# A second layer fed in groups of 1, 1, 2, 2 and 2 row tiles, with all engines' orders rewritten there

## The reference

```python
def _L1_ffn_ref(x, w_gate, w_up, w_down, up_reorder_index, down_reorder_index):
    xf = x.reshape(B * S, H)                                       # 1024 rows of 256
    qx, sx, sc = _reorder_quantize_x(xf, up_reorder_index)         # row scale, e4m3 rounding
    g = _qlinear(qx, sx, sc, w_gate, up_reorder_index, out_idx=down_reorder_index)
    u = _qlinear(qx, sx, sc, w_up, up_reorder_index, out_idx=down_reorder_index)
    t = jax.nn.silu(g) * u                                         # 1024 rows of 704
    qt, st, sct = _reorder_quantize_x(t, down_reorder_index)
    return _qlinear(qt, st, sct, w_down, down_reorder_index).reshape(B, S, H)
x = x + _L1_ffn_ref(_L1_cond_ref(x, ...), ...)                     # cond: sigmoid(x) * ratio
```

## Time and profile before

| | |
|---|---|
| runs | 673.81 us median of 3 (673.74 to 676.32) |
| profiled execution | 671.21 us, of which its span is 669.3 us |
| granted TensorE clock, mean | 0.93 |
| busy in the span | PE 508.7, DVE 511.1, ACT 356.4, POOL 262.0 us |

### The profile page before, as it was taken

How to read it: one execution, slowest core, us unless ns; L and a number is a source line. 1 busy time by engine, 2 the same in 40 slices (tenths; PEclk the granted TensorE clock), 3 DMA queues, 4 the chain that set the end, 5 groups by cost and what they waited for, 6 DMA issues and landing times.

```text
span 669.3 us, 9350 instructions
## 1 busy us (share of the span) xinstructions
PE 508.7 (76%) x3050; PEld 347.1 (52%) x3050; DVE 511.1 (76%) x964; ACT 356.4 (53%) x758; POOL 262.0 (39%) x212
## 2 busy tenths in 40 slices
PE   2011298799999999997489989899999998046663
PEld 1000133478888888876146646566656665024432
DVE  4999867788888888874459769869798787379772
ACT  3226235777777778763054545644734564256542
POOL 4465014744444445415460872633350600630001
PEclk9999999899999999997599979999999999577785
DMA  8200003030000000004903831441453100210000
GB/s 278 96 0 0 0 1 125 27 140 1 1 1 1 1 1 25 9 1 144 292 25 107 269 58 36 163 101 43 164 147 116 25 24 16 82 53 8 17 17 24
DMA packets 28363, 44.24 MB, mean 66 GB/s; under 512 B 4795, under 2 KB 21435, under 8 KB 28059
## 3 DMA queue, kind: packets, MB, share of 16 engines
q1 hardware_dynamic: 20843, 31.43, 14.2%
q0 software_dynamic: 3072, 8.14, 5.3%
q10 hardware_dynamic: 4400, 4.06, 1.8%
HBM read 38.51 MB, written 5.12 MB: 65 GB/s over the span
## 4 chain that ended last, share of the span: by engine, by line
PE 50%; DVE 26%; ACT 8%; issue 8%; POOL 5%; DMA 1%; SPq 0%; DVEq 0%; ACTq 0%; POOLq 0%; PEldq 0%
PE pw L419 9%; PE pb L419 8%; PE pb L607 7%; PE sc L460 5%; PE sc L607 5%; PE po L419 4%; PE pt L471 3%; DVE areg L1104 2%; PE sc L683 2%; PE pb L683 2%; DVE areg L1090 2%; DVE areg L1088 2%; PE pt L616 1%; POOL breg L1668 1%; DVE areg L1451 1%
## 5 line engine op out<-in xcount | busy, mean ns | idle before, releaser
L607 PE MATMUL pb<-wreg,areg 128*128 x184 | 83.7, 598 | 0.9 <-ACT areg L925 0.8
L1640 POOL TENSOR_TENSOR breg<-breg,con 128x512 f32<-128x512 f32 x32 | 40.7, 1271 | 80.3 <-ACT breg L824 80.3
L419 PE MATMUL pw<-areg 128*128 128x256 f16 x406 | 58.8, 280 | 7.7 <-DVE areg L1459 7.7
L607 PE MATMUL sc<-wreg,areg 128*128 x184 | 63.2, 486 | 0.0
L419 PE MATMUL pb<-areg,wreg 128*128 128x512 f16 x240 | 58.9, 382 | 2.0 <-ACT breg L824 1.9
L832 ACT ACTIVATE breg<-breg,mx 128x128 f32<-128x128 f32 (+1 forms) x128 | 56.6, 446 | 1.6 <-DVE mx L1212 1.6
L460 PE MATMUL sc<-areg,breg 128*128 128x128 f32 (+1 forms) x256 | 48.8, 335 | 5.6 <-DVE mx L1212 4.3
L607 PEld LDWEIGHTS pb<-wreg,areg 128*128 128x128 f32 x184 | 33.6, 193 | 35.4 <-issue 35.1
L419 PEld LDWEIGHTS pw<-areg 128*128 128x128 f16 x406 | 40.3, 100 | 17.9 <-DVE areg L1459 11.2
L1635 POOL TENSOR_TENSOR breg<-breg 128x512 f32<-128x512 f32 x32 | 44.4, 1388 | 4.5
L460 PEld LDWEIGHTS sc<-areg,breg 128*128 128x128 f32 x256 | 38.9, 195 | 13.2 <-POOL breg L1635 4.2
(11 more groups left out here) (247 smaller groups left out, 1293.8 us busy)
## 6 DMA issues: line engine op xcount, KB each, us to landing
wreg<-in_L_ffn_w SPq DMA_DIRECT2D x24, 896.0 KB, 8.5
ys_dram<-areg ACTq DMA_DIRECT2D x23, 128.0 KB, 1.7
wreg<-in_L_ffn_wq SPq DMA_DIRECT2D x1, 2048.0 KB, 8.6
wreg<-in_L_ffn_wo SPq DMA_DIRECT2D x1, 2048.0 KB, 8.3
areg<-in_fside_BxSxS ACTq DMA_DIRECT2D x4, 256.0 KB, 5.4
x_in<-in_x SPq DMA_DIRECT2D x4, 256.0 KB, 3.9
h_dram<-areg SPq DMA_DIRECT2D x8, 128.0 KB, 1.7
out_dram<-areg SPq DMA_DIRECT2D x8, 128.0 KB, 1.7
```

The source lines that it names most:

```text
L419: last = nc.tensor.matmul(bank, w(a), m(b), start=first and k == 0, stop=final and k == 2)
L607: last = nc.tensor.matmul(bank, xsT[:, parity, c * P:(c + 1) * P], wreg[:, bass.ds(base + (m * C + c) * FF + lo, w)], start=c == 0, stop=c ...
L1640: G.tensor_tensor(t2[:, parity, :].rearrange("p (b n) -> p b n", b=2), t2[:, parity, :].rearrange("p (b n) -> p b n", b=2), rope_sin.rearr ...
```

## The change

The rows of the second layer come in five groups, of 1, 1, 2, 2 and 2 row tiles, in place of four pairs. Each group has its own semaphore for its gathers, and GpSimd issues all gathers without a wait between them. The sigmoid and the mixed input get buffers for all eight tiles; qxT, qtT, tscaled and traised are doubled. TensorE no longer follows one loop: gate and up products are two functions, the first three tiles have an order of their own, and from tile 3 on a pass holds the products of tile i, the inner transposes of tile i - 2 and the down products of tile i - 3. Products of zeros stand in six places of TensorE's order. ScalarE's and VectorE's orders are written out anew, and ScalarE takes one silu of a single column ahead of tile 2. In the first layer, one half of the last ratio piece moves: TensorE makes it in the last expert tile's pass, in the bank po, where no next tile's transposes stand.

```diff
+GROUPS = ((0, 1), (1, 1), (2, 2), (4, 2), (6, 2))
-        qxT = cut(areg, 4736, D // 2, F16).rearrange("p (c n) -> p c n", c=C)
+        qxT = cut(areg, 8576, D, F16).rearrange("p (k c n) -> p k c n", k=2, c=C)
...
-                      19: piece(down, 1, 0), 22: piece(ratio, 3, 0), 23: piece(ratio, 3, 1)}
+                      19: piece(down, 1, 0), 22: piece(ratio, 3, 1)}
...
                 if n + 1 < MT:
                     x_transposes(n + 1, (n + 1) % 4, x_slot.get(n))
+                elif n < MT:
+                    pe.wait_ge(s["xT_copied"], MT)
+                    ratio_piece(B - 1, 0, po).then_inc(s["xT_done"], 1)
...
+            pe.wait_ge(s["hTlo_done"], MT)
+            pe.wait_ge(s["x1_ready"], 1)
+            keep_clock(pt2[:, 1, :], 10)
+            quantised_transposes(0)
+            gate_products(0)
+            quantised_transposes(1)
+            up_products(0)
+            gate_products(1)
+            up_products(1)
+            keep_clock(pt2[:, 1, :], 10)
+            inner_transposes(0)
+            keep_clock(pt2[:, 1, :], 16)
+            quantised_transposes(2)
+            gate_products(2)
+            up_products(2)
+            quantised_transposes(3)
+            for i in range(3, NT):
+                gate_products(i)
+                up_products(i)
+                if i + 1 < NT:
+                    quantised_transposes(i + 1)
+                inner_transposes(i - 2)
+                down_quantised(i - 3)
+                keep_clock(pt2[:, 1, :], 2)
+            inner_transposes(NT - 2)
+            down_quantised(NT - 3)
+            keep_clock(pt2[:, 1, :], 3)
+            down_quantised(NT - 2)
+            inner_transposes(NT - 1)
+            keep_clock(pt2[:, 1, :], 4)
+            down_quantised(NT - 1)
...
             def copy_qxT(i):
                 act.wait_ge(s["qxT_done"], i + 1)
-                if i >= 1:
-                    act.wait_ge(s["upp_done"], i)
+                if i >= 2:
+                    act.wait_ge(s["upp_done"], i - 1)
...
             input_gate(0)
             scaled_input(0)
             input_gate(1)
+            copy_qxT(0)
             scaled_input(1)
-            input_gate(2)
-            copy_qxT(0)
             gate_of_tile(0)
             copy_qxT(1)
             gate_of_tile(1)
...
+            scaled_inner(0)
+            input_gate(2)
+            scaled_inner(1)
+            copy_qtT(0)
+            scaled_input(2)
+            input_gate(3)
+            input_gate(4)
+            nc.scalar.activation(tf[:, 1, 0:1], ident[:, 0:1], ACT.Silu)
+            copy_qxT(2)
+            gate_of_tile(2)
+            copy_qxT(3)
+            scaled_input(3)
+            gate_of_tile(3)
+            scaled_inner(2)
+            copy_qxT(4)
+            copy_qtT(1)
+            scaled_input(4)
+            for j in range(2, NT):
+                if j + 1 < NT:
+                    scaled_inner(j + 1)
+                if j + 2 < NT:
+                    gate_of_tile(j + 2)
+                if j + 3 < NT:
+                    copy_qxT(j + 3)
+                copy_qtT(j)
...
             mix_input(1)
+            round_input(1)
             combine(2)
-            round_input(1)
             inner_rows(0)
...
+            inner_rows(1)
+            round_inner(0)
+            mix_input(2)
+            combine(3)
+            combine(4)
+            round_input(2)
+            round_inner(1)
+            mix_input(3)
+            inner_rows(2)
+            mix_input(4)
+            round_input(3)
+            inner_rows(3)
+            round_inner(2)
+            output_rows(0)
+            round_input(4)
+            for i in range(4, NT):
+                inner_rows(i)
+                round_inner(i - 1)
+                output_rows(i - 3)
+            round_inner(NT - 1)
+            for i in range(NT - 3, NT):
+                output_rows(i)
...
-            gather_pair(0)
-            gather_pair(1)
-            for p in range(2):
-                pool.wait_ge(s_g[p], 64)
-                gather_pair(p + 2)
+            for g in range(len(GROUPS)):
+                gather_group(g)
```

More of the change, by code:

```diff
@@ L660, in quantised_transposes @@
             def quantised_transposes(i):
-                pe.wait_ge(s["qx_ready"], i // 2 + 1)
+                group = [g for g, (first, count) in enumerate(GROUPS) if first <= i < first + count][0]
+                pe.wait_ge(s["qx_ready"], group + 1)
                 if i >= 1:
@@ L668, in quantised_transposes, with first_products, gate_products @@
                 last.then_inc(s["qxT_done"], 1)
-            def gate_up(i):
+            def first_products(i, m):
+                for k in range(2):
+                    bank = (sc2[:, k] if m == 0 else pb[k])[:, 0:IH]
+                    for c in range(C):
+                        for a in range(2):
+                            last = nc.tensor.matmul(bank, qxT[:, i % 2, c, :], w_fold[m][:, a, c, k * IH:(k + 1) * IH],
+                                                    start=c == 0 and a == 0, stop=c == C - 1 and a == 1)
+                last.then_inc(s["gatep_done" if m == 0 else "upp_done"], 1)
+            def gate_products(i):
                 pe.wait_ge(s["qxT_copied"], i + 1)
@@ L675, in gate_up, with up_products @@
                     pe.wait_ge(s["inner_b_done"], MT)
[L676 to L685, removed]
+                first_products(i, 0)
+            def up_products(i):
+                if i >= 1:
+                    pe.wait_ge(s["inner_ready"], i)
+                first_products(i, 1)
             def inner_transposes(i):
@@ L1011, in gate_of_tile @@
                 act.wait_ge(s["gatep_done"], i + 1)
+                group = [g for g, (first, count) in enumerate(GROUPS) if first <= i < first + count][0]
+                act.wait_ge(s["xout_ready"], group + 1)
                 if i >= 2:
@@ L1018, in scaled_inner, with copy_qtT @@
                 act.wait_ge(s["inv_ready"], i + 1)
[L1019 to L1022, removed]
+                if i >= 2:
+                    act.wait_ge(s["qt_ready"], i - 1)
+                nc.scalar.activation(tscaled[i % 2], tvals[i % 2], ACT.Copy, scale=rs[:, 8, i:i + 1])
+                nc.scalar.activation(traised[i % 2], tvals[i % 2], ACT.Copy, scale=rs[:, 9, i:i + 1]).then_inc(s["scaled_ready"], 1)
+            def copy_qtT(i):
+                act.wait_ge(s["qtT_done"], i + 1)
+                if i >= 2:
+                    act.wait_ge(s["dn_done"], i - 1)
+                nc.scalar.copy(qtT[i % 2][0:IQ, :, :], pt2[0:IQ, 0, :].bitcast(F16).rearrange("p (c n) -> p c n", c=NI)).then_inc(s["qtT_copied"], 1)
             input_gate(0)
@@ L1548, in round_inner @@
                     dve.wait_ge(s["qtT_done"], i)
-                nearest_e4m3(qt[:, :], tscaled, traised, tgrid).then_inc(s["qt_ready"], 1)
+                nearest_e4m3(qt[:, :], tscaled[i % 2], traised[i % 2], tgrid).then_inc(s["qt_ready"], 1)
             def output_rows(i):
```

125 lines of the change are left out of this document (49 added, 76 removed).

## The result

The changed kernel takes 666.9 us (median of 4 runs, 665.85 to 668.35) against 673.77 us (672.29 to 676.32) for the kernel before, run beside it: a ratio of 0.9896, interval 0.9858 to 0.9933. It is faster, by 6.9 us (1.0%, clear of the noise), and just inside the range of the prediction; but 13.3 us was forecast. The profiled execution took 667.76 us, with a span of 666.0; the forecast for it was 658.4. So the question is where some 9 us stayed.

What follows compares the result with a forecast made beforehand. VectorE bounds the second layer: 576.15 + 66.4 - 1.5 + 2.0 + 2.3 + 0.4 + 5.45 = 651.2, against 663.99: -12.8, 658.4 us profiled; with 2.1 for the runs' median, 660.5 us, range 655.5 to 667.

Steps and rivals of the forecast that it cites:

- What VectorE still waits for: Second layer: VectorE's remaining waits, 2.0 us in front, 2.3 for TensorE's clock, 0.4 in the last tiles.
- crossings between engines 0.3: Second layer, first tile's way from combine to rounded input: handovers between engines take 0.3 of its 5.5 us.
- First combine: Second layer's start: one tile needs two gathers, not four, -2.55 us, start at 576.15; gathers' lost waits worth nothing.
- a dear split (+2.9): Upper bound, VectorE in the second layer: splitting into five groups costs its upper bound, +2.9 us.
- two more tiles at 1.2 GHz (+2.3): Upper bound, TensorE in the second layer: two further tiles' products run at 1.2 GHz, +2.3 us.
- late zeros (+1): Upper bound, TensorE's queue: products of zeros delay the transposes queued behind them, +1 us.
- The first layer's end: End of the first layer: moving the half ratio gives -0.3 us, bounds -0.8 and 0.
- stay at 1.2 GHz: Rival, TensorE in the second layer: zeros take time without raising the clock; 677 us, chance 0.05.
- the ring: Rival, second layer: ScalarE's strict order holds up the last five tiles, 6.5 us each; 667 us, chance 0.12.
- the first two gathers were enough: Against the rival, second layer's start, that two gathers land no sooner than four did: +2.55, 663 us, chance 0.04.
- The rival of gathers slowed by VectorE: Second layer: VectorE passes hold each of the last thirteen gathers, the fifth combine waits 6 us; 666 us, chance 0.03.
- The last part: Second layer's end: from the last rounding to the end of the last addition, 5.45 us, kept as before.

Runs made afterwards that it cites:

- the pause: The changed kernel with GpSimd's last eight gathers held until VectorE has rounded the second tile: 657.99 us, ratio 0.9783 to the kernel before.

## Why the prediction was right in sign and half wrong in size

**What failed** is a part of two steps. "What VectorE still waits for" gave the front 2.0 us, with "crossings between engines 0.3" in the first tile's way; "First combine" took the waits that GpSimd loses between gathers as "nothing". Both looked at the gathers' own pace, which did stay at 1.28 us. Neither asked what else runs while sixteen of them run: the change put TensorE's first signals into that run, and they came up to 8 us late. The hole, 7.7 us on VectorE, is the missing term; shown by the pause, with which the stage from first combine to last addition takes 73.1 us (577.68 to 650.78) in place of 82.4 (578.23 to 660.64); 75.05 was forecast. One of the prediction's own signs shows it too: VectorE was to be busy 9 tenths or more up to the last rounding, and was for 61.09 of 77.25 us from 577, or 0.79; with the pause it is 61.08 of 66.76 us from the first combine, or 0.91.

**That the time lay in the range was luck.** The upper bound, 667, was made of a dear split (+2.9), two more tiles at 1.2 GHz (+2.3) and late zeros (+1). The split cost less than forecast, one more tile had 1.2 GHz and cost 1.2 us, the zeros cost half a microsecond at most. What filled the range is the hole, which is in none of its terms.

**The first layer's end** was off as well: the first gather at 574.08, due at 572.03. By rows, the move itself did what was said (-0.3), and more (-0.55): the down products follow the last subtraction by 0.05 us (567.19 - 566.59 - 0.55), where before they stood 0.33 us behind it, after the ratio piece of the earlier trace rows (566.71 - 565.83 - 0.55), and the copy before the last store (0.27 on the path) is gone. But the 21 products took 4.00 us in place of 2.46, at 1.2 GHz, as in one of the two profiles of the kernel before. The rest, 0.76 us, is that the first layer came to its last subtraction later (566.59 against 565.83). The sum was made on an execution whose clock held there; the 2.1 us kept for the runs' median covered such things, but not by name.

**What was right.** The combine started 1.9 us behind its second gather's end (576.37 to 578.23). From combine to gate products took 6.25 us, forecast 6.45. VectorE's work is 62.45 us, forecast 63.0: nine instructions more cost little, near the line through the two widths. In the late loop the period is 5.06 us, forecast 5.2, with 2.4 GHz granted from 630 to 649. Two tiles had 1.2 GHz, as counted (clock 0.55 and 0.58 in the windows at 612 and 626); there VectorE waited 0.57 us for a silu (616.90) and 0.34 for up products (630.71), where 2.3 was taken. A third, not counted, is the second tile behind the hole: its gate and its up products took 2.53 us each, and VectorE waited 1.20 us for the latter (600.11). The zeros cost little: the first ten ended at 583.80, 0.4 us behind the rounded input (583.40), one of the prediction's signs of being wrong, but the transposes started at 583.60, at most 0.2 us late, and leaving the ten out changed nothing that the noise lets one see. Two zeros also stand ahead of the gate products of the tile at 626, so the 0.34 us may be theirs. The last part, 6.4 us for 5.45, was short by 0.9: the last inner transposes (656.46) stand behind the down products of the tile ahead, which took 1.86 us from 654.79.

**The rivals.** TensorE did not stay at 1.2 GHz; the ring is gone, and the first two gathers were enough. The rival of gathers slowed by VectorE gave 666 us, almost the measured time, and for another cause: the pace stayed at 1.28 us. The rule of the Trainium skill in "SBUF — State Buffer", section "Who interferes with whom", does not show as a block here: the two gathers beside VectorE's third combine took 1.07 and 1.10 us, most of the others 0.95. What the gathers disturbed was another engine's signals.

**What stays open.** What holds the signals is not shown. Nor is where between eight and sixteen gathers it begins: in the profile after and with the ratio put back the first late signal was due with ten gathers issued, in the first profile of the kernel before one was prompt with thirteen. It ends when the gathers do: in the profile after the DMA engines are busy 0.56 of the time from 595.0 to 595.5 and not at all from there on, and the last two signals come within a microsecond. A lateness in the records alone can't be it, as the waiting engines themselves start late. Whether the recording of a run has a part in it can't be told from these runs, all of which were recorded. The price of the moved ratio by itself wasn't measured, for the clock's sake.

## What to carry to other kernels

When a change brings work forward, list what ran beside it before and what will run beside it now, engine by engine; a stream that was harmless because nobody needed an answer during it can be the new bound. A wait for "remote" whose producer ended long before can be a late signal, not a missing order. Here re-ordering around it gave nothing in two tries; finding what ran until it ended, and breaking that up, did. And a stage ahead of the change needs its own range where its clock differs between two profiles of one kernel.

## What was not expected of the hardware

In seven traces with sixteen indirect gathers issued 1.28 us apart, several semaphore signals of TensorE came 1 to 8 us late, until about 2 us after the last issue, while VectorE's to ScalarE and to TensorE stayed prompt; a pause of 3.5 us after the eighth gather kept TensorE's on time. Not every signal in such a run is late: one with thirteen gathers issued was prompt. The 21 last down products of the first layer take between 2.46 and 4.13 us from one profiled execution to the next, by where the granted clock falls to 0.50.
